# Expert tiles of a two-layer transformer block: TensorE's loop over tiles takes three tiles per pass

## What is computed

```python
probs = jax.nn.softmax(xf @ router_w.T, axis=-1)
topv, topi = jax.lax.top_k(probs, 2)
topv = topv / (topv.sum(axis=-1, keepdims=True) + 1e-09)
cw = (jax.nn.one_hot(topi, e, dtype=xf.dtype) * topv[..., None]).sum(axis=1)
h = jax.nn.gelu(jnp.einsum('td,edh->teh', xf, w1), approximate=False)
y = jnp.einsum('teh,ehd->ted', h, w2)
out = jnp.einsum('te,ted->td', cw, y)
```

## Time and profile before

| | us |
|---|---|
| median of 3 runs | 1315.61 |
| lowest and highest | 1308.95, 1320.06 |
| the profiled execution | 1316.48 |
| its span, first to last instruction | 1314.7 |

### The profile page before, as it was taken

One profiled execution on the slowest core, in us unless ns is written; L12 is line 12 of the kernel. 1 busy time (PEld: TensorE's weight loads), 2 busy tenths in 40 slices (PEclk: granted clock), 3 DMA queues, 4 the chain that ended last, 5 costly groups with the idle time before them and its releaser, 6 DMA issues. The chain is left out here.

```text
span 1314.7 us, 26291 instructions
## 1 busy us (share of the span) xinstructions
PE 1038.9 (79%) x8436; PEld 707.5 (54%) x8437; DVE 750.1 (57%) x1748; ACT 546.7 (42%) x910; POOL 489.8 (37%) x553
## 2 busy tenths in 40 slices
PE   6248777887887425999999999999915888895996
PEld 4124445454454314888888888888802344442453
DVE  3656777777664695444444444444437877734552
ACT  1125666566554332333333333333303555551663
POOL 0056565565540002333332222222168866401441
PEclk9656898999888556999999999999956999998998
DMA  4031222222213431111111111111142222000112
GB/s 107 7 94 45 61 65 66 71 74 69 64 52 99 141 102 42 49 48 48 48 48 48 48 47 39 46 44 48 40 118 80 77 61 73 21 1 0 26 49 57
DMA packets 70696, 76.37 MB, mean 58 GB/s; under 512 B 18733, under 2 KB 63648, under 8 KB 70624
## 3 DMA queue, kind: packets, MB, share of 16 engines
q1 hardware_dynamic: 63808, 56.83, 14.4%
q0 software_dynamic: 6816, 18.62, 5.5%
HBM read 52.28 MB, written 23.12 MB: 57 GB/s over the span
## 5 line engine op out<-in xcount | busy, mean ns | idle before, releaser
L1226 DVE CAST hh_e<-h_e 128x512 f16<-128x512 f32 x156 | 66.3, 425 | 240.2 <-ACT h_e L1204 150.3
L1158 PE MATMUL up_ps<-xT_e,experts 128*128 128x256 f16 x624 | 171.8, 275 | 8.2 <-issue 6.6
L1159 PE MATMUL up_ps<-xT_e,experts 128*128 128x256 f16 x624 | 171.4, 275 | 0.0
L1160 PE MATMUL up_ps<-xT_e,experts 128*128 128x256 f16 x624 | 171.4, 275 | 0.0
L1172 PE MATMUL y_ps<-experts,hh_e 128*128 x624 | 170.1, 273 | 0.1
L1173 PE MATMUL y_ps<-experts,hh_e 128*128 x624 | 170.1, 273 | 0.0
L1174 PE MATMUL y_ps<-experts,hh_e 128*128 x624 | 170.1, 273 | 0.0
L1204 ACT ACTIVATE h_e<-up_ps 128x512 f32<-128x512 f32 x156 | 93.2, 597 | 173.3 <-PE up_ps L1160 173.3
L496 POOL TENSOR_TENSOR bd<-keys,blocks 128x616 f16<-128x616 f16 x128 | 155.0, 1232 | 8.1 <-PE s_ps L568 6.2
L1099 POOL COPY idx_e<-token 128x2 int32 (+1 forms) x39 | 25.5, 654 | 326.2 <-PE xT_ps_e L1143 264.5
L1228 DVE TENSOR_TENSOR hh_e<-h_e,hh_e 128x512 f16<-128x512 f32 x156 | 108.1, 693 | 5.4
(11 more groups left out here) (252 smaller groups left out, 2236.2 us busy)
## 6 DMA issues: line engine op xcount, KB each, us to landing
experts<-in_L_ffn_w SPq DMA_DIRECT2D x22, 512.0 KB, 4.0
y_scratch<-y_e SPq DMA_DIRECT2D x39, 256.0 KB, 3.0
experts<-in_x SPq DMA_DIRECT2D x256, 32.0 KB, 1.8
w_r<-in_L_ffn_w SPq DMA_DIRECT2D x10, 512.0 KB, 3.8
x_scratch<-experts SPq DMA_DIRECT2D x32, 128.0 KB, 1.8
xh_scratch<-experts SPq DMA_DIRECT2D x32, 128.0 KB, 1.8
x_a<-x_scratch SPq DMA_DIRECT2D x32, 128.0 KB
out<-out_f SPq DMA_DIRECT2D x128, 32.0 KB, 1.6
```

The source lines that it names most:

```text
L1158: mm(out, w[0], xT[0][:, c, :], start=c == 0, stop=False)
L1159: mm(out, w[0], xT[1][:, c, :], start=False, stop=False)
L1160: last = mm(out, w[1], xT[0][:, c, :], start=False, stop=c == DC - 1)
L1226: nc.vector.tensor_copy(hh[0][:, q % 2, :], h[:, q % 2, :]).then_inc(hhi_ok, 1)
```

## The change

Only TensorE's list changes. The expert read moves out of `step` into a function `place`, which returns the offset. TensorE no longer uses `tiles`: it does tile 0, then a loop of (39 - 3) / 3 = 12 passes with three tiles each (1 + 3i, 2 + 3i, 3 + 3i). At the head of a pass it reads the three experts, one after the other, into three registers, and then does the three steps. Tiles 37 and 38 follow the loop as straight-line code, each with its own read in front. The other engines keep their loops, and the semaphores keep their counts.

```diff
-                def step(k, more):
+                def place(k):
+
                     expert = pe.value_load(G["tile_expert"][0:1, ds(k, 1)], min_val=0, max_val=E - 1)
-                    at = pe.snap(expert * (8 * HID))
+                    return pe.snap(expert * (8 * HID))
+
+                def step(k, at, more):
                     W = G["experts"]
...
                 transpose(0)
-                tiles(pe, step)
+                step(0, place(0), True)
+                with pe.Fori(0, (ET - 3) // 3) as i:
+                    first = [1 + i * 3 + j for j in range(3)]
+                    at = [place(k) for k in first]
+                    for k, a in zip(first, at):
+                        step(k, a, True)
+                step(ET - 2, place(ET - 2), True)
+                step(ET - 1, place(ET - 1), False)
```

## The result

The changed kernel takes 1331.91 us (median of 6 runs, 1326.99 to 1337.32) against 1315.98 us of the kernel before in the same runs: ratio 1.0126, 95% interval 1.009 to 1.0162. It is slower by 16 us. 1324 was forecast; the time lies inside the range of 1312 to 1347, and just above the 1317 to 1331 that the prediction gave its own case.

The account below looks back on a forecast made before the run. TensorE's own stream was taken to bound the expert tiles, with 12.8 us lost at boundaries. Saved branches -8.6, uncovered reads +15.4 and index arithmetic +1.3 gave +8.1 us, hence 1324 us, range 1312 to 1347.

Parts of the forecast that it names:

- its own case: Whole kernel: serial reads at heads outweigh the branches saved; 1324 us, own range 1317 to 1331, chance 0.64.
- The reading of the boundary: Between tiles: read plus taken branch outlast the sequencer's 1.1 us lead over the array; 0.35 us each, 12.8 us total.
- Fewer branches: 24 boundaries inside passes lose nothing, and tile 36's exit has no taken branch; 8.6 us gained.
- I take their loss as 0: 24 boundaries inside passes: about 0.3 us of wait registers fits under the sequencer's 1.1 us lead; 8.3 us gained.
- Neither takes the place.: Inside tiles: neither VectorE's transposed-row half nor the lightly busy ScalarE and GpSimd becomes the next late wait; no loss.
- Three reads at the head: Heads of 12 passes: two of three serial reads are uncovered, 0.64 us each; 15.4 us lost.
- the index arithmetic: Heads of passes: one extra FUSED_REGOPS for tile numbers, 0.11 us per head; 1.3 us, bounds 0 to 5.
- Sum: Whole kernel: -8.6 + 15.4 + 1.3 = +8.1 us.
- the clock: Rival at pass heads: TensorE's clock falls in the longer idle; 20 us on top, 1344 us, chance 0.07.
- the refetch: Rival at 11 taken branches: the pass's code is fetched again, 2.6 us each; 29 us, 1353 us, chance 0.17.
- Slower by over 1%: Whole kernel: time above 1329 us, chance 0.29.
- cheap in a row: Rival at pass heads: extra reads overlap and cost less than alone; 1315 or 1307 us, chance 0.12.

Follow-up runs that it names:

- e6: Kernel before with all of TensorE's tiles as straight-line code, each expert read in front of its tile, gathers unchanged: 1316.6 us, ratio to before 0.9993.
- e7: Kernel before with TensorE's tiles as straight-line code and GpSimd's row-number copy made a tile ahead, so gathers issue earlier: 1305.2 us, ratio to before 0.9899.
- e2: Changed kernel with GpSimd's copy of the row numbers made a tile ahead, so both gathers issue earlier: 1323.9 us, ratio to before 1.0063.
- e3: Kernel before with GpSimd's copy of the row numbers made a tile ahead, so both gathers issue earlier: 1314.8 us, ratio to before 0.9989.
- e10: Kernel before with each tile's expert read twice at its head, the second value being used: 1344.3 us, ratio to before 1.0219.
- e9: Changed kernel with each expert read in front of its own tile and twelve tiles per pass: 1322.4 us, ratio to before 1.0078.
- e4: Kernel before with GpSimd's gathers waiting for ScalarE's copy of the transposed rows instead of the transposes: 1324.7 us, ratio to before 1.0047.
- e4b: Kernel before with GpSimd's gathers waiting for VectorE's low half of the transposed rows: 1327.6 us, ratio to before 1.012, two runs only.
- e8: Changed kernel with each expert read in front of its own tile and six tiles per pass: 1314.3 us, ratio to before 0.9979.

## Why the prediction was right, and where it was short

- *The reading of the boundary.* Right: the gap is the sequencer's, read plus branch against a head of start of 1.1 us. e6 and e7 keep one read per tile, drop the branch, and all 38 boundaries are at the pace. In e7 the stage shortens by 13.2 us, where 12.8 were said to be all there is, and the boundaries lost 12.7.
- *Fewer branches, "I take their loss as 0".* Right at the boundary itself: 0.11 us at all 24.
- *"Neither takes the place."* Wrong, the step that failed. Two waits were looked at, for the transposed rows and for the emptied result. That ScalarE and GpSimd are busy a third of the time or less was taken as a reason, and a busy share says nothing of a chain that has to end by a given moment. The next late thing is down(0)'s wait for the first gelu's low half. In the kernel before these were the subtraction that makes it and the start of down(0):

```profile
563.28 0.69 DVE L1228 TENSOR_TENSOR hh_e<-h_e,hh_e 128x512 f16<-128x512 f32 x1
...
564.29 0.27 PE L1172 MATMUL y_ps<-experts,hh_e 128*128 x1
```

The subtraction ended at 563.97, and down(0) started on time 0.32 us later. Where it is late that takes 0.24 us (609.61 to 609.85). So there were 0.08 us of slack. Up(0) moved 0.35 us towards GpSimd's gathers, its semaphore came 0.38 us later relative to its matmuls, and 0.29 us were lost on average: in 24 tiles 7.0 us, most of what the branches had given. e2 and e3 show that moving the gathers alone takes it away.
- *Three reads at the head.* Right: serial, 0.64 us for one more (e10). One FUSED_REGOPS for a pass was taken for the index arithmetic, the bounds held two; it is two, and the head's own is 68 ns in place of 50. The 12 heads cost 1.81 us each above the pace where 1.74 was forecast, and all boundaries together 9.1 us more, where the sum had 8.1.
- *Sum.* 8.1 forecast, 16 measured: 1.0 of the difference is the heads, 7.0 is down(0). The mechanism of the heads was right, and half of the slowdown came from a wait that the prediction put at nothing. The case forecast had a range of its own of 1317 to 1331, and the time is above it; it lies in the range to 1347 only because that was drawn wide for the clock and the refetch, and neither happened. That part is luck. "Slower by over 1%", which is what came, had been given 0.29.
- *Two slips without weight.* TensorE is at nine tenths in three slices near the end of the earlier trace rows, 36, 38 and 39, not in two. With nothing left of the two reads, -8.6 + 1.3 from 1315.6 gives 1308, not 1307.
- *The rivals.* The refetch did not happen at this size (44 packets, branches of 215 ns). The clock stayed at 1.00 in all 11 passes through idles of 1.63 us; in e9 it fell behind one of 3.8. The reads were not cheap in a row: one more cost 0.64 us at each boundary (e10).

## What to carry to other kernels

A register read on TensorE's sequencer is free only while the array has queued work to cover it: one read per tile under a head start of 1.1 us cost nearly nothing, three in a row cost the two uncovered ones in full. Put it where the sequencer waits for a semaphore anyway. And before pricing a removed gap, look at the tightest wait behind it in the same tile, with its slack in hundredths of a microsecond, and at what is timed by the tile before (here the gathers): that doesn't move along.

## What the runs showed of the hardware that was not expected

- TensorE's semaphore for a finished `up` comes 0.29 us after its last matmul's start at the full clock. When it is due in the half microsecond behind the end of a GpSimd gather issue, it comes only about 0.55 us after that end. Over all 13 traces this holds for 237 of the 239 that fell due there: they came 0.24 to 0.66 us behind the end, most of them 0.53 to 0.63. It is 0.45 us after the start with an issue ending 0.09 ahead of the start (before), 0.65 with 0.11 after it (e4), 0.83 with 0.27 after it (changed), and 0.29 with the issue over 0.5 ahead (e2). With the issue still running (e4b) it is 0.29 in 24 tiles and 0.54 to 0.61 in 12. ScalarE's semaphore for the emptied result isn't held: in e2, where its second instruction ends 0.26 to 0.31 us behind the second issue's end in most tiles, SyncE's next record follows within 0.11 us in every tile. Why TensorE's is held was not found.
- GpSimd's multiplication stretches VectorE's cast from 0.43 to 1.26 us where they meet (e4b). The Trainium skill (SBUF — State Buffer, section on the two separate sides) says that the port pair the two engines share is an exclusive lock, held for a whole instruction, against VectorE's two-port modes and its instructions with two inputs in SBUF. The trace agrees: in the tile shown the cast ends at 608.53, 0.29 us behind the multiplication's end at 608.24, and it is 0.29 to 0.30 us in all 16 such tiles, though the cast starts anywhere from 0.14 to 0.58 us after the multiplication. That this cast uses a two-port mode is not shown.
- A taken branch of TensorE stays at 0.22 us with a body of 1590 instructions (e8) and takes 3.7 us with one of 3180 (e9).
